# Cross-attention of a decoder layer: key tiles scored in pairs, another order of the work beside them, ten batches per loop iteration

## The chip, the cores and the metric

The kernel runs on one core of one Trainium2 chip. The metric is the time of one execution on the device in microseconds. The core's engines are TensorE (PE in the profile; its weight loads are PEld), VectorE (DVE), ScalarE (ACT), GpSimd (POOL), and SyncE (SP), which here only issues DMAs.

## The reference, cut to what matters

The layer is self-attention, cross-attention and a feed-forward block, each with a residual and a layernorm after it. The change is in the middle one. For 32 batches, 100 queries and 1444 keys of 256 features, 16 heads of 16:

```python
def _w8a8_linear(x, w, b):            # both sides rounded to whole numbers in -127..127
    qx, sx = _dyn_quant(x)
    qw, sw = _quant_weight(w)
    y = jnp.einsum('bnc,oc->bno', qx, qw) * (sx * sw[:, 0])
    return y + b
q = _w8a8_linear(x, wq, bq).reshape(B, N, H, D).transpose(0, 2, 1, 3)
k = (cond @ wk.T + bk).reshape(B, L, H, D).transpose(0, 2, 1, 3)
v = (cond @ wv.T + bv).reshape(B, L, H, D).transpose(0, 2, 1, 3)
scores = jnp.einsum('bhnd,bhld->bhnl', q, k) * inv_sqrt_d + mask[:, None]
attn = jax.nn.softmax(scores, axis=-1)
o = jnp.einsum('bhnl,bhld->bhnd', attn, v)
return _w8a8_linear(o.transpose(0, 2, 1, 3).reshape(B, N, C), wo, bo)
```

## The kernel before, in words

The three stages follow each other. Cross-attention works on one batch per turn. Its 1444 keys are 12 tiles of up to 128 (the last has 36 rows), its 16 heads four quads. A **unit** `("u", g, t)` is one key tile for one quad: four score matmuls with keys on the partitions (L1283), one exponential on ScalarE over 128 x 400 (L1098), and, two units later, four matmuls that add the weighted values to `acc` (L1246). There are 48 units in a turn. Scores go by turns into two PSUM banks, `unit0` and `unit1`, and exponentials into three slots of `prob`. Between the first and second score matmul of a unit TensorE branches on a flag that tells whether the mask is zero (L1287).

Keys and queries are float32 cut into three bf16 parts, stacked over 96 partitions; three more rows hold the negated row maximum, so that the scores come out already lowered. So the maxima must be known before the scores: for each head, `mh` (two matmuls of 512 keys) and `ml` (one of 420) make scores with queries on the partitions in `ca_rowmax` (L1163), VectorE reduces them (L1388), and per quad VectorE cuts the maximum in three parts, `mr` transposes these into a `unit` bank (L1172), and ScalarE copies them into the query stack (L1081).

Besides its own units a turn prepares the next batch and finishes the one before. `slots` names the tasks behind each unit, and every engine goes through the same list (`run_turns`), doing its part of each task:

- `ct` k c: four context tiles transposed on TensorE (L1210), copied by ScalarE (L1047).
- `kp` k c: key product of a third of the keys (L1129; its first half is `ka`); ScalarE writes the high part (L1056), VectorE the rest (L1347), `km` is ScalarE's middle part (L1063), and GpSimd makes the low part (L1002).
- `vp` j: value product of two tiles (L1136; first half `va`), with the bias added by VectorE into `ca_vaug` (L1362).
- `qq`, `qx`, `qp`, `qs`: quantise the next queries (VectorE), transpose, multiply, cut into parts on GpSimd, transpose the parts.
- `ma`, `mf`: is the next mask zero.
- `eo`, `ex`, `ey`: output of the batch before: divide and quantise, transpose, output product, residual and layernorm.

SP works through `step` once per batch: it loads the next context, then copies key parts from `ca_key_part` into the stack `ca_ks` as they become ready (L887, 24 copies), and doubles parts inside the stack (L893, L895), for heads 0 to 7 and then 8 to 15. `mh` 0 and `mh` 8 wait for these. It also loads queries, mask and residual and stores the result.

The counters of `Banks` order who writes and who frees a PSUM bank. The loop over batches holds two turns per iteration; the first and the last turn stand outside it, so it runs 15 times.

Of the kernel before, what the change touches and what calls it, by code (L numbers as in the profile page):

```python
# [19 lines left out]
P = 128  # L20
# [4 lines left out]
class Banks:  # L25
# [614 lines left out]
def cross_attention(nc, sems, x1, ctx_in, mask, wq, bq, wkT, bk_in, wvT, bv, wo, bo, x2):  # L640
# [48 lines left out]
    UNITS = NQ * TILES  # L689
    LAG = 2  # L690
    HALF = EARLY = H // 2
    slots = {}

    def place(u, *tasks):
        slots.setdefault(u, []).extend(tasks)
# [4 lines left out]

    place(-1, ("ct", 0, 0), ("ct", 0, 1))
    place(1, ("eo",), ("ka", 0, 0), ("kp", 0, 0))
    place(3, ("km", 0, 0), ("ct", 1, 0), ("ex",))
    place(4, ("ka", 0, 1), ("kp", 0, 1), ("ey",))
    place(5, ("ct", 1, 1))
    place(6, ("km", 0, 1))
    place(7, ("ka", 1, 0), ("kp", 1, 0), ("mh", 8))  # L710
    place(8, ("km", 1, 0))
    place(9, ("ml", 8), ("ka", 1, 1), ("kp", 1, 1), ("mr", 1))
    place(10, ("mh", 9), ("km", 1, 1), ("ct", 2, 0))
    place(11, ("ct", 2, 1), ("mh", 10))
    place(12, ("ml", 9), ("ka", 2, 0), ("kp", 2, 0))
    place(13, ("qq",), ("ml", 10), ("mh", 11))
    place(14, ("ka", 2, 1), ("kp", 2, 1))
    place(15, ("ml", 11))
    place(16, ("km", 2, 0), ("km", 2, 1), ("mh", 12))
    place(17, ("qx",), ("ml", 12), ("qp",))  # L720
    place(18, ("mh", 13), ("va", 0), ("vp", 0))
    place(19, ("ml", 13))
    place(20, ("mh", 14))
    place(21, ("ml", 14), ("va", 1), ("mr", 2), ("vp", 1))
    place(23, ("mh", 15), ("qs", 0))
    place(24, ("va", 2), ("ml", 15), ("vp", 2))
    place(25, ("qs", 1))
    place(27, ("mh", 0))
    place(28, ("va", 3))
    place(29, ("ml", 0), ("mh", 1), ("vp", 3))  # L730
    place(31, ("ml", 1), ("mh", 2))
    place(33, ("ml", 2), ("va", 4))
    place(34, ("mr", 3), ("mh", 3), ("vp", 4))
    place(36, ("ml", 3))
    place(37, ("mh", 4), ("va", 5), ("vp", 5))
    place(38, ("ma",))
    place(39, ("ml", 4))
    place(41, ("mh", 5))
    place(43, ("ml", 5))
# [1314 lines left out]
```

## Time and profile before

| | us |
|---|---|
| median of 3 runs | 4297.15 (4296.39 to 4300.14) |
| span of the profiled execution | 4293.6 |
| TensorE busy | 3851.9 (90%) |
| VectorE busy | 2586.9 (60%) |
| ScalarE busy | 1705.4 (40%) |
| GpSimd busy | 646.0 (15%) |

"Busy" adds up the instructions of an engine. The granted clock is the share of TensorE's full clock that it was given; 0.50 is 1.2 GHz and 1.00 is 2.4 GHz. "Issue" as a releaser means that the engine waited for nothing that the profile shows.

### The profile page before, as it was taken

The page shows a single profiled execution, that of the slowest core. Times are in us where ns is not written, and L with a number is a line of the kernel's source. Part 1 is how long each engine was busy: PE and PEld are TensorE (multiplying, and loading weights), DVE is VectorE, ACT ScalarE, POOL GpSimd, SP SyncE. Part 2 cuts the span into 40 slices and gives each one's busy share as a digit, 9 for nine tenths or more (in the row PEclk, how much of TensorE's full clock was granted, in tenths as well). Part 3 has the DMA queues.
Part 4 walks back from the last instruction along what each step waited for, and adds up shares of the span by engine and source line. Part 5 has one row for each costly group of instructions (what it writes and reads, how often), then busy time and mean ns, then how long its engine had stood idle before and what let it go on. Part 6 is the DMA issues. An engine that isn't in the chain of part 4 may idle for free. (4 is left out here: it accounts for less than half of the span.)

```text
span 4293.6 us, 98259 instructions
## 1 busy us (share of the span) xinstructions
PE 3851.9 (90%) x34364; PEld 2651.9 (62%) x34364; DVE 2586.9 (60%) x6225; ACT 1705.4 (40%) x3482; POOL 646.0 (15%) x784
## 2 busy tenths in 40 slices
PE   7999999966989889889889988988988987999998
PEld 6999999963555555555555555555555545666665
DVE  4444444454667666666666666666756745666665
ACT  3223222222444444444444544544544433333232
POOL 0000000021111011011111110110101102243222
PEclk9999999987999899999999999989999968999999
DMA  2000000014635436446445354454453411000000
GB/s 91 13 12 11 11 11 11 8 38 77 105 74 103 86 71 110 84 80 103 77 88 100 71 103 88 83 95 86 88 97 74 86 28 54 16 11 11 19 11 12
DMA packets 121851, 257.48 MB, mean 60 GB/s; under 512 B 18564, under 2 KB 99276, under 8 KB 118364
## 3 DMA queue, kind: packets, MB, share of 16 engines
q1 hardware_dynamic: 113136, 243.95, 30.2%
q10 hardware_dynamic: 8300, 7.69, 0.6%
q8 instruction: 297, 4.87, 0.5%
q14 instruction: 118, 0.97, 0.1%
HBM read 99.79 MB, written 9.83 MB: 26 GB/s over the span
## 5 line engine op out<-in xcount | busy, mean ns | idle before, releaser
L1388 DVE CUSTOM_DVE_ANT_0 ca_rowmax<-ca_rowmax,ca_msk 100x1024 f32<-100x1024 f32 (+1 forms) x1024 | 926.9, 924 | 460.9 <-PE ca_rowmax L1163 452.7
L1098 ACT ACTIVATE ca_prob<-ca_unit 128x400 f32<-128x400 f32 (+1 forms) x1536 | 759.0, 501 | 824.6 <-PE ca_unit L1283 802.4
L1163 PE MATMUL ca_rowmax<-ca_ks,ca_qs 96*100 96x512 bf16 (+1 forms) x1536 | 518.5, 407 | 155.9 <-DMA ca_ks<-ca_ks 78.3
L1283 PEld LDWEIGHTS ca_unit<-ca_qs,ca_ks 99*128 99x128 bf16 (+1 forms) x6144 | 413.5, 102 | 280.9 <-issue 177.7
L1246 PE MATMUL ca_acc<-ca_prob,ca_vaug 128*17 128x100 f32 x12288 | 576.9, 262 | 0.0
L1283 PE MATMUL ca_unit<-ca_qs,ca_ks 99*128 99x100 bf16 (+1 forms) x6144 | 569.3, 216 | 1.3 <-issue 0.3
L1002 POOL TENSOR_TENSOR ca_key_part<-ca_key_rest,ca_key_part 128x512 bf16<-128x512 f32 (+1 forms) x192 | 209.7, 1099 | 2028.8 <-ACT ca_key_part L1063 2028.8
L1136 PE MATMUL ca_ring<-ca_wvT,ca_ctxT 128*128 128x256 f32 (+1 forms) x1536 | 441.8, 419 | 0.4 <-DVE ca_vaug L1362 0.4
L1129 PE MATMUL ca_ring<-ca_ctxT,ca_wkT 128*128 128x512 f32 (+1 forms) x768 | 365.7, 600 | 3.9 <-DVE ca_key_rest L1347 2.2
L1163 PEld LDWEIGHTS ca_rowmax<-ca_ks,ca_qs 96*100 96x100 bf16 x1536 | 157.6, 128 | 323.3 <-issue 213.3
L1136 PEld LDWEIGHTS ca_ring<-ca_wvT,ca_ctxT 128*128 128x128 f32 (+1 forms) x1536 | 297.8, 202 | 84.1 <-issue 27.6
L1246 PEld LDWEIGHTS ca_acc<-ca_prob,ca_vaug 128*17 128x17 f32 x12288 | 205.8, 96 | 139.7 <-issue 14.4
L1347 DVE SCALAR_TENSOR_TENSOR ca_key_rest<-ca_ring,ca_bk_col,ca_key_part 128x512 f32<-128x512 f32 (+1 forms) x192 | 137.8, 717 | 190.1 <-ACT ca_key_part L1056 190.1
L1056 ACT ACTIVATE ca_key_part<-ca_ring,ca_bk_col 128x512 bf16<-128x512 f32 (+1 forms) x192 | 127.0, 661 | 245.3 <-PE ca_ring L1129 245.3
L313 ACT ACTIVATE sa_capped<-sa_ps 100x400 f32<-100x400 f32 x128 | 64.5, 504 | 402.3 <-PE sa_ps L419 402.3
L1210 PE MATMUL ca_ring<-ca_ident,ca_ctx 128*128 128x128 f32 (+1 forms) x768 | 138.5, 304 | 90.0 <-issue 86.9
L1129 PEld LDWEIGHTS ca_ring<-ca_ctxT,ca_wkT 128*128 128x128 f32 x768 | 140.9, 198 | 109.0 <-issue 104.2
L1210 PEld LDWEIGHTS ca_ring<-ca_ident,ca_ctx 128*128 128x128 f32 (+1 forms) x768 | 98.1, 153 | 136.6 <-issue 124.5
L86 PE MATMUL sa_ps<-sa_xT_hi,sa_w_hi 128*128 128x400 f32 x512 | 177.3, 346 | 0.0
L88 PE MATMUL sa_ps<-sa_xT_hi,sa_w_lo 128*128 128x400 f32 x512 | 175.0, 342 | 0.0
L259 POOL TENSOR_SCALAR_AFFINE_SELECT sa_causal<-sa_prob 100x400 f32<-100x400 f32 x128 | 69.3, 542 | 701.8 <-ACT sa_prob L320 701.8
L516 DVE COPY sa_kT<-sa_ps 128x400 f32<-128x400 f32 x128 | 73.5, 574 | 168.3 <-PE sa_ps L88 168.3
(258 smaller groups left out, 6549.7 us busy)
## 6 DMA issues: line engine op xcount, KB each, us to landing
ca_ks<-ca_key_part SPq DMA_DIRECT2D x768, 90.2 KB, 4.2
ca_ks<-ca_ks SPq DMA_DIRECT2D x64, 722.0 KB, 5.8
ca_ctx<-in_ctx SPq DMA_DIRECT2D x32, 1408.0 KB
ca_ks<-ca_ks SPq DMA_DIRECT2D x64, 361.0 KB, 8.8
ca_msk<-in_mask_BxSxS_ff SPq DMA_DIRECT2D x32, 564.1 KB
sa_w_stage<-in_L_attn_w_qkv SPq DMA_DIRECT2D x12, 512.0 KB, 5.2
sa_x_in<-in_x ACTq DMA_DIRECT2D x8, 400.0 KB
sa_x_res<-in_x SPq DMA_DIRECT2D x8, 400.0 KB
```

The lines of the kernel that those rows point to most:

```text
L86: pe.matmul(out, w_hi, x_hi, start=(start and n == 0), stop=False)
L88: last = pe.matmul(out, w_lo, x_hi, start=False, stop=(stop and n == len(pairs) - 1))
L1002: pool.tensor_tensor(key_part[:, 2, c, s], key_rest[:, n % 2, 0:w], key_part[:, 1, c, s], ALU.subtract).then_inc(parts_out, 1)
L1098: act.activation(prob[0:rows(t), u % 3, :], unit[bank][0:rows(t), 0:QUAD * N], ACT.Exp)\
L1129: return pe.matmul(ring[bn.bank(task)][:, 0:w], wkT_s[:, ci, c * P:(c + 1) * P], ctxT[:, ci, s], start=(ci == 0), stop=(ci == C - 1))
L1136: last = pe.matmul(ring[bn.bank(task)][0:rows(t), j * D:(j + 1) * D], ctxT[:, ci, t * TL:t * TL + rows(t)], wvT_s[:, ci, :], start=(ci == ...
L1163: last = pe.matmul(rowmax[0:N, s0:s1], qs[0:STACK, par, h, :], ks[0:STACK, par, h, s0:s1], start=True, stop=True)
L1210: last = pe.transpose(tile[:, n * TL:n * TL + rows(t)], ctx_t[0:rows(t), t, c * P:(c + 1) * P], ident[0:rows(t), 0:rows(t)])
L1246: last = pe.matmul(acc[32 * j:32 * j + DH + 1, g * N:(g + 1) * N], vaug[0:rows(t), par, t, head_at(g * QUAD + j), :], prob[0:rows(t), u % ...
L1283: return pe.matmul(unit[bank][0:rows(t), j * N:(j + 1) * N], ks[:, par, h, s], qs[:, par, h, :], start=(j == 0), stop=True, skip_group_che ...
L1347: dve.scalar_tensor_tensor(key_rest[:, n % 2, 0:w], ring[bank][:, 0:w], bk_col[:, c:c + 1], key_part[:, 0, c, s], ALU.add, ALU.subtract)\
L1388: dve.tensor_tensor_reduce(rowmax[0:N, s0:s1], rowmax[0:N, s0:s1], msk[:, par, s0:s1], 1.0, -3.0e38, ALU.add, ALU.max, top[:, bank, h:h + ...
```

## The change: what it does

It touches cross-attention alone.

- **Rounds of two tiles.** A turn has 24 pairs `("u", p)` in place of 48 units. `unit` becomes one PSUM tensor over two banks and is counted as one buffer, which the pairs and the `mr` tasks share. Eight score matmuls fill it, the branch on the mask stands ahead of the eighth, one activation over 128 x 800 makes the exponentials (two activations where the second tile has 36 rows), and the eight value matmuls of the pair before follow directly. `prob` has four slots.
- **Order of the tasks.** The `slots` table is written anew over rounds 0 to 24. The key products stand in rounds 1 to 8 (of 24), the value products in rounds 9 to 20. Their two halves are one task each, so `ka` and `va` are gone. Heads 0 to 5 of the next batch are scored for their maxima in rounds 16 to 23, heads 6 and 7 at the start of their own turn (before: 0 to 7 ahead of it). `mr` 1, 2, 3 and 0 stand in rounds 5, 11, 17 and 23, and rounds 12, 18 and 21 hold only `ml` 13, 1 and 3.
- **The end of a batch.** `ez` is new: the last layernorm step, in round 6, two rounds behind `ey`. The result is written in place (`res = summed`), so VectorE waits in `eo` until the batch before is stored.
- **Loop.** Ten turns per iteration, 3 iterations. Tasks that have no batch at the first and last turn are passed over by `skip_run`, which sets the counters.

SP's program is the same but for the count of pairs.

```diff
+    slots = {
+        ...
+        11: [("mr", 2), ("qx",), ("mh", 13), ("vp", 1), ("qp",)],
+        12: [("ml", 13)],
+        ...
+    }
-        unit = [ctx.enter_context(nc.psum_tensor(f"ca_unit{k}", [P, 512], F32)) for k in range(2)]
+        unit = ctx.enter_context(nc.psum_tensor("ca_unit", [P, 2, 512], F32))
-        bc = Banks(nc, sems, "ca_cur", cur_order, lambda t: cur_order.index(t) % 2)
+        bc = Banks(nc, sems, "ca_cur", cur_order, lambda t: 0, lag={t: 1 - batch_of(t) for t in cur_order})
-        prob = sb("prob", [TL, 3, QUAD * N])
+        prob = sb("prob", [TL, 4, QUAD * N])
-        res = sb("res", [N, 1, D])
+        res = summed
+        LOOP = 10
-            with eng.Fori(0, B // 2 - 1) as pair:
-                turn(2 * pair + 1, 1)
-                turn(2 * pair + 2, 0)
+            with eng.Fori(0, (B - 2) // LOOP) as n:
+                for k in range(LOOP):
+                    turn(LOOP * n + k + 1, (k + 1) % 2)
...
             def do_round(b, par, p):          # ScalarE
+                t, s = 2 * (p % PER_QUAD), slice(2 * (p % 2), 2 * (p % 2) + 2)
+                bc.wait_full(act, ("u", p), b)
+                if rows(t + 1) == TL:
+                    act.activation(prob[:, s, :], unit[:, :, 0:QUAD * N], ACT.Exp).then_inc(bc.freed[0], 1)
+                else:
+                    act.activation(prob[:, s.start, :], unit[:, 0, 0:QUAD * N], ACT.Exp)
+                    act.activation(prob[0:rows(t + 1), s.start + 1, :], unit[0:rows(t + 1), 1, 0:QUAD * N],
+                                   ACT.Exp).then_inc(bc.freed[0], 1)
...
             def do_round(b, par, p):          # TensorE
-                head(0)
+                for j in range(QUAD):
+                    head(0, j)
+                for j in range(QUAD - 1):
+                    head(1, j)
                 with pe.If(masked[par] != 0):
...
-                for j in range(1, QUAD):
-                    last = head(j)
-                last.then_inc(bc.filled[bank], 1)
-                if u >= LAG:
-                    weighted_values(b, par, u - LAG)
+                head(1, QUAD - 1).then_inc(bc.filled[0], 1)
+                if p:
+                    weighted_values(b, par, p - 1)
...
                 elif kind == "eo":            # VectorE
+                    dve.wait_ge(out_stored, 16 * b + 1)
...
                 elif kind == "ey":
-                    dve.wait_ge(out_stored, 16 * b + 1)
+                elif kind == "ez":
                     layernorm_apply(dve, summed, moments, rstd, res, 1, rstd_done, out_ready, b)
```

On TensorE, in the first turn, where `mr` 1 stands, before: two units (scores, branch, values), `ml` (100x420), a key product, `mr` into `unit1`, and the next scores into `unit0`.

```order
L1283 MATMUL ca_unit1<-ca_qs,ca_ks 128x100 x3
L1246 MATMUL ca_acc<-ca_prob,ca_vaug 17x100 x4
L1283 MATMUL ca_unit0<-ca_qs,ca_ks 128x100
L1287 COMPARE_AND_BRANCH
L1288 MATMUL ca_unit0<-ca_ident,ca_msk 128x400
L1287 UNCONDITIONAL_BRANCH
L1283 MATMUL ca_unit0<-ca_qs,ca_ks 128x100 x3
L1246 MATMUL ca_acc<-ca_prob,ca_vaug 17x100 x4
L1163 MATMUL ca_rowmax<-ca_ks,ca_qs 100x420
L1129 MATMUL ca_ring1<-ca_ctxT,ca_wkT 128x512 x2
L1172 MATMUL ca_unit1<-ca_ident_b,ca_top_part 3x100 x4
```

The same place now, round 5 (its second tile has 36 rows):

```order
L1283 MATMUL ca_unit<-ca_qs,ca_ks 128x100 x4
L1283 MATMUL ca_unit<-ca_qs,ca_ks 36x100 x3
L1290 COMPARE_AND_BRANCH
L1292 MATMUL ca_unit<-ca_ident,ca_msk 128x400
L1292 MATMUL ca_unit<-ca_ident,ca_msk 36x400
L1290 UNCONDITIONAL_BRANCH
L1283 MATMUL ca_unit<-ca_qs,ca_ks 36x100
L1246 MATMUL ca_acc<-ca_prob,ca_vaug 17x100 x8
L1168 MATMUL ca_unit<-ca_ident_b,ca_top_part 3x100 x4
L1159 MATMUL ca_rowmax<-ca_ks,ca_qs 100x512 x2
L1132 MATMUL ca_ring1<-ca_ctxT,ca_wkT 128x512 x2
```

Eight scores stand together, eight values behind them, and `mr` writes `unit` right behind these, which is the buffer that the eight scores have just filled.

On VectorE, around the quantising of the next queries (`ca_x_q` to `ca_x_int`), before. The rows that write `ca_rowmax` are the maxima of `mh` (100x1024) and `ml` (100x420).

```order
L1347 SCALAR_TENSOR_TENSOR ca_key_rest<-ca_ring0,ca_bk_col,ca_key_part 128x420
L632 TENSOR_REDUCE ca_x_st<-ca_x_q 100x1
L633 TENSOR_SCALAR ca_x_st<-ca_x_st 100x1
L634 RECIPROCAL ca_x_st<-ca_x_st 100x1
L635 TENSOR_SCALAR ca_x_sc<-ca_x_q,ca_x_st 100x256
L636 TENSOR_SCALAR ca_x_sc<-ca_x_sc 100x256
L637 TENSOR_SCALAR ca_x_int<-ca_x_sc 100x256
L1388 ISA ca_rowmax,ca_top<-ca_rowmax,ca_msk 100x420
L1388 ISA ca_top 100x1
L1388 ISA ca_rowmax,ca_top<-ca_rowmax,ca_msk 100x1024
```

And now, in round 10:

```order
L1391 ISA ca_rowmax,ca_top<-ca_rowmax,ca_msk 100x1024
L1391 ISA ca_top 100x1
L644 TENSOR_REDUCE ca_x_st<-ca_x_q 100x1
L645 TENSOR_SCALAR ca_x_st<-ca_x_st 100x1
L646 RECIPROCAL ca_x_st<-ca_x_st 100x1
L647 TENSOR_SCALAR ca_x_sc<-ca_x_q,ca_x_st 100x256
L648 TENSOR_SCALAR ca_x_sc<-ca_x_sc 100x256
L649 TENSOR_SCALAR ca_x_int<-ca_x_sc 100x256
L1391 ISA ca_rowmax,ca_top<-ca_rowmax,ca_msk 100x420
L1391 ISA ca_top 100x1
```

Ahead of it stands the maximum of `mh` 12 in place of a key rest, and only `ml` 12 is queued behind it before the next round.

## Rows read from the trace of the kernel before

**Rows 1.** The page: its span, and two groups of its part 5.
```profile
span 4293.6 us, 98259 instructions
...
L1246 PE MATMUL ca_acc<-ca_prob,ca_vaug 128*17 128x100 f32 x12288 | 576.9, 262 | 0.0
L1283 PE MATMUL ca_unit<-ca_qs,ca_ks 99*128 99x100 bf16 (+1 forms) x6144 | 569.3, 216 | 1.3 <-issue 0.3
```

**Rows 2.** Stretches: length, busy time by engine, granted clock, DMA share, GB/s.
```profile
1046.00:3529.00 2483.00, 2240.06 (x24324) 1343.10 (x24322) 1612.64 (x3865) 1167.23 (x2345) 304.64 (x341) 0.92 0.48 86
1138.04:1212.93 74.89, 69.14 (x767) 41.49 (x766) 51.17 (x123) 36.77 (x75) 9.84 (x12) 0.95 0.52 93
1212.93:1295.41 82.48, 70.41 (x767) 42.72 (x766) 51.39 (x123) 36.90 (x75) 9.85 (x12) 0.92 0.46 85
```

**Rows 3.** Timeline of SP's queue: context loads, first and last of 29.
```profile
1138.04 0.41 SPq L874 DMA_DIRECT2D ca_ctx<-in_ctx  x1
...
3336.51 0.40 SPq L874 DMA_DIRECT2D ca_ctx<-in_ctx  x1
```

**Rows 4.** TensorE's waits from 1117 to 3340: us in total, times, longest.
```profile
PE ca_ring L1210 <- issue: 86.9, 28, 4.1
PE ca_rowmax L1163 <- DMA ca_ks<-ca_ks: 72.0, 24, 4.5
PE ca_rowmax L1163 <- DVE ca_top L1388: 54.9, 56, 1.8
```

**Rows 5.** Timeline of TensorE at a loop end: start, length, [idle before].
```profile
1587.08 0.47 PE L1210 MATMUL ca_ring<-ca_ident,ca_ctx 128*128 128x128 f32 x1 [4.13 <-issue]
1590.00 1.76 PE L1210 MATMUL ca_ring<-ca_ident,ca_ctx 128*128 128x128 f32 x7 [2.46 <-issue]
```

**Rows 6.** Stretches behind a wait for VectorE and at that loop end.
```profile
1541.05:1544.46 3.41, 3.41 (x19) 2.16 (x19) 2.09 (x4) 0.50 (x1) 2.71 (x4) 0.50 1.02 149
1585.42:1595.66 10.24, 6.13 (x24) 4.21 (x25) 2.41 (x9) 1.99 (x4) 0.00 (x0) 0.50 0.07 24
```

**Rows 7.** Timeline of TensorE at the wait for a maximum.
```profile
1539.95 0.64 PE L1163 MATMUL ca_rowmax<-ca_ks,ca_qs 96*100 96x512 bf16 x2 [1.69 <-DVE ca_top L1388]
```

**Rows 8.** Timeline of TensorE without a wait, at the full clock.
```profile
1545.08 0.63 PE L1163 MATMUL ca_rowmax<-ca_ks,ca_qs 96*100 96x512 bf16 x2
1545.55 0.35 PE L1283 MATMUL ca_unit<-ca_qs,ca_ks 99*128 99x100 bf16 x4
1545.83 0.37 PE L1246 MATMUL ca_acc<-ca_prob,ca_vaug 128*17 128x100 f32 x8
1546.12 0.38 PE L1163 MATMUL ca_rowmax<-ca_ks,ca_qs 96*100 96x420 bf16 x1
1546.34 1.03 PE L1136 MATMUL ca_ring<-ca_wvT,ca_ctxT 128*128 128x256 f32 x4
1547.30 0.34 PE L1172 MATMUL ca_unit<-ca_ident_b,ca_top_part 100*3 100x100 bf16 x4
1547.57 1.13 PE L1136 MATMUL ca_ring<-ca_wvT,ca_ctxT 128*128 128x256 f32 x4
```

**Rows 9.** Timeline of all engines: a unit's scores and their exponential.
```profile
1578.77 0.34 PE L1283 MATMUL ca_unit<-ca_qs,ca_ks 99*128 99x100 bf16 x4
...
1579.23 0.50 ACT L1098 ACTIVATE ca_prob<-ca_unit 128x400 f32<-128x400 f32 x1 [0.15 <-PE ca_unit L1283]
```

**Rows 10.** Groups by form, ScalarE, 1117 to 3340: busy, mean ns of one.
```profile
L1074 ACT ACTIVATE ca_qs<-ca_ring 96x800 bf16<-96x800 bf16 x56 | 46.6, 832 | 23.8 <-PE ca_ring L1233 23.8
```

**Rows 11.** Timeline: last high part, SP's copies and doublings, first `mh`.
```profile
1533.81 0.61 ACT L1056 ACTIVATE ca_key_part<-ca_ring,ca_bk_col 128x420 bf16<-128x420 f32 x1 [1.32 <-PE ca_ring L1129]
...
1534.61 10.89 SPq L887 DMA_DIRECT2D ca_ks<-ca_key_part  x16
1547.88 0.52 SPq L893 DMA_DIRECT2D ca_ks<-ca_ks  x1
...
1557.53 0.63 PE L1163 MATMUL ca_rowmax<-ca_ks,ca_qs 96*100 96x512 bf16 x2 [2.22 <-DMA ca_ks<-ca_ks]
```

More of the change, by code:

```diff
@@ L57, in skip, with skip_run @@
         pe.sem_inc(self.freed[self.bank(tile)], 1)
+    def skip_run(self, pe, tiles, turn_of):
+        first, n = {}, {}
+        for tile in tiles:
+            bank = self.place[tile][0]
+            first.setdefault(bank, tile)
+            n[bank] = n.get(bank, 0) + 1
+        for bank, tile in first.items():
+            self.wait_empty(pe, tile, turn_of(tile))
+            pe.sem_inc(self.filled[bank], n[bank])
+            pe.sem_inc(self.freed[bank], n[bank])
     def wait_empty(self, eng, tile, turn):
@@ L711, in cross_attention @@
[L711 to L721, printed above, removed]
@@ L769, in cross_attention @@
+    cur_order = [t for t in timeline if t[0] in ("u", "mr")]
+    top_order = [t for t in timeline if t[0] in ("mh", "ml", "eo", "ex", "ey")]
     with ExitStack() as ctx:
@@ L952, in _, with run_turns, turn @@
             sp.wait_ge(out_stored, 16 * B + 1)
-        def run_turns(eng, do_task, do_round, skip=lambda task, turn: None):
-            def turn(b, par, first=False, last=False):
-                for u in ROUNDS:
-                    do_round(b, par, u)
-                    for task in slots.get(u, []):
+        LOOP = 10
+        assert (B - 2) % LOOP == 0 and LOOP % 2 == 0
+        def run_turns(eng, do_task, do_round, skip=lambda tasks, turn: None):
+            def turn(b, par, aheads=(-1, 0, 1)):
+                for p in ROUNDS:
+                    if 0 in aheads:
+                        do_round(b, par, p)
+                    for task in slots.get(p, []):
@@ L960, in turn @@
                         ahead = batch_of(task)
-                        if ahead == -1 and first:
-                            skip(task, -1)
-                        elif not (ahead == 1 and last):
+                        if ahead in aheads:
                             do_task(b + ahead, (par + ahead) % 2, task)
-            for task in timeline:
-                if batch_of(task) == 1:
-                    do_task(0, 0, task)
-            turn(0, 0, first=True)
-            with eng.Fori(0, B // 2 - 1) as pair:
-                turn(2 * pair + 1, 1)
-                turn(2 * pair + 2, 0)
@@ L973, in run_turns @@
-            turn(B - 1, 1, last=True)
-            for n in range(EARLY):
-                skip(("mh", n), B)
-            for task in end_tasks:
+                        elif ahead == -1:
+                            skip([task], b)
+            skip([t for t in timeline if batch_of(t) < 1], -1)
+            for p in ROUNDS:
+                for task in slots.get(p, []):
+                    if batch_of(task) == 1:
+                        do_task(0, 0, task)
+            turn(0, 0, aheads=(0, 1))
@@ L977, in run_turns @@
+            with eng.Fori(0, (B - 2) // LOOP) as n:
+                for k in range(LOOP):
+                    turn(LOOP * n + k + 1, (k + 1) % 2)
+            turn(B - 1, 1, aheads=(-1, 0))
+            ends = [t for t in timeline if batch_of(t) == -1]
+            skip([t for t in timeline if batch_of(t) == 1], B - 1)
+            skip(timeline[:timeline.index(ends[0])], B)
+            for n, task in enumerate(ends):
                 do_task(B - 1, 1, task)
+                if n + 1 < len(ends):
+                    skip(timeline[timeline.index(task) + 1:timeline.index(ends[n + 1])], B)
```

203 lines of the change are left out of this document (82 added, 121 removed), and 23 rows, old and new, of the table slots.

## The prediction, made before the changed kernel ran

> **What bounds the kernel now.** I read the busy time by stretch first, then the starts of the batches, then TensorE's waits, then its timeline at the waits, and last the queues that those waits name.
>
> The change touches only cross-attention. That stage is 2483 us of the 4293.6 us span [rows 1, 2]. In it TensorE is busy 2240 us, at a mean granted clock of 0.92, while VectorE has 1613 us and ScalarE 1167 us. So TensorE sets the pace, and what can be won is its idle time, its time at the lower clock, and the price of each of its steps.
>
> The load of the context tile is issued at the same place of every batch. From its row at 1138.04 to that at 3336.51 there are 28 batches, so 78.5 us each [rows 3]. They are not alike: one takes 74.89 us, the next 82.48 [rows 2]. The longer one has the end of the loop body in it. There TensorE stands still for 4.13 us and, one matmul later, for 2.46 us, with nothing that it waits for [rows 5]. The grouped row counts 86.9 us in 28 such places, two at each of 14 loop ends, so 6.2 us per end [rows 4]. Behind such a halt the granted clock is 0.50, which is 1.2 GHz, for 10.24 us, of which 6.13 us are work [rows 6]; at 2.4 GHz that work takes half, so 3.1 us more are lost. A loop end costs 6.2 + 3.1 = 9.3 us. Without one a batch is 78.5 - 9.3/2 = 73.8 us.
>
> In those 73.8 us TensorE waits 72.0/28 = 2.6 us for the stacked keys and 54.9/28 = 2.0 us for VectorE's row maxima [rows 4]. After such a wait (1.69 us here) the clock is 0.50 for 3.41 us [rows 6, 7], which costs 1.7 us of work; with two such waits in a batch, 3.4 us. Waits and their clock: 8.0 us a batch.
>
> **The change, part by part.**
>
> *Loop ends.* Two turns per iteration become ten: 15 iterations become 3, 14 loop ends become 2. Saved: 12 x 9.3 = 112 us. From below, with the idle time alone, it is 12 x 6.2 = 74 us; from above I see nothing dearer, since a batch's code streams once either way. In the second turn of today's body (74.89 us) no such halt shows, so ten turns in a row should show none.
>
> *Groups of eight.* Today four score matmuls start 0.28 us ahead of the value matmuls, and those 0.29 us ahead of the next step [rows 8]. Four scores span 0.35 us and one lasts 0.216 [rows 1, 8], so they start (0.35 - 0.216)/3 = 0.045 us apart; four such steps are 0.18, and 0.10 is left for the change to another group. The values span 0.37 with 0.262 for one, two passes some 0.11 apart, so 0.07 to 0.09 is left there. A pair of tiles drops one of each: 0.57 x 2 - 0.18 = 0.96 us instead of 1.14, and 24 pairs save 4.3 us a batch. The bounds are 0 (if the gap is the price of the weights, and not of the group) and 4.6. I take 4.0. Joining the two halves of the key and value products changes an order only, and I put it at nothing, as no work of theirs goes.
>
> *One score buffer in place of two.* The scores of a pair can be written only when the exponential of the pair before has been read out. ScalarE began 0.12 us after the scores' end (1578.77 + 0.34 to 1579.23) [rows 9]. An activation of 800 columns takes 0.832 us [rows 10], where today two of 400 take 0.50 each. Counted from the first score: last one starts at 7 x 0.045, ends 0.21 later, so 0.53; then 0.12 + 0.83; the buffer is free at 1.48. TensorE has scores and values for 0.96, so a round needs 0.5 us of other tasks to hide it. A matmul pair "mh" is 0.47, "ml" 0.22, a value product 2 x 0.96 [rows 8]. Most rounds have enough. Rounds 12, 18 and 21 hold one "ml" alone: 3 x (0.5 - 0.22) = 0.8 us. The four "mr" transposes now share that buffer and stand right behind the values: 4 x 0.5 = 2.0 us. Together +2.8 us a batch; the bounds are 0 (if ScalarE is quicker than the row of 800) and 24 x 0.5 = 12 us (no cover at all).
> The Trainium skill (Perfetto Trace Analysis, Matmuls) says that independent matmul groups should rotate through PSUM banks, so that read-out of one overlaps the next group. By that rule the one buffer is a loss in every round. The rows agree with the delay, but the tasks between the rounds are such other work.
>
> *Keys early, values late.* The chain behind the first "mh 0" is long: the last key product's high part is written at 1533.81 + 0.61 = 1534.42, SP then issues 16 copies (10.89 us), the two doubling copies follow at 1547.88, and the "mh" that needs them starts at 1557.53, after a wait of 2.22 us [rows 11]. That is 23.1 us from the high part, or 23.8 from the end of the product on TensorE (0.12 + 0.61 more). SP's program is the same, so this stays. After the change what lies between is rounds 9 to 15 and the pair of 16: eight pairs at 0.96 = 7.7, five "ml" 1.1, four "mh" 1.9, four value products 7.7, one "mr" 0.3, the query steps about 1.2 (an estimate from 20 short matmuls at the pitches above): 19.9 us. With waits of 0.5 (mr 2) and 0.3 (round 12), and 1.2 at the query transpose (below), 21.9. So about 1.9 us of wait stay, with one spell of the low clock, 1.7.
> VectorE quantises the queries in round 10, behind the maximum of mh 12, and the transpose that needs it stands in round 11, not four rounds on. I put 1.2 us there, between 0 and the 1.69 that TensorE waits behind the same work today [rows 7]. Queued behind that wait are mh 13 and value product 1. VectorE is busy 51.2 us in a batch [rows 2], so 0.73 of 70: tight, and 0.6 us of small waits for maxima in rounds 20 and 0 are added. The last layernorm step is a task of its own two rounds later, so VectorE no longer stands for GpSimd; off TensorE's path, nothing. The load of the mask flag had eight transposes to hide it and now stands ahead of the first scores: 0.3.
> Waits and clock after: 1.9 + 1.7 + 1.2 + 0.6 + 0.3 = 5.7, against 8.0: saved 2.3.
>
> **The sum.** A batch: -4.0 + 2.8 - 2.3 = -3.5 us, so 70.3. But the 0.8 us of score-buffer wait inside the key chain are already in its 1.9, and I do not take them out: they stand for what I have not seen. 31 turns hold all this work: 31 x 3.5 = 108 us. Of the other turn and the head of the stage nothing is counted; to be cautious I take 100. 4293.6 - 112 - 100 = 4082 us of span. The shown median is 4297.15, 3.5 above the span of the profiled execution, so 4085 us.
>
> **The rivals.**
> 1. *The body breaks even.* The group change is worth 0 to 1, and the buffer and VectorE eat it; only loop ends are won: 4297 - 112 = 4185. For it: VectorE at 0.73 and a chain of 23.8 us that no order shortens. Against it: the wait total of 8.0 us shrinks by the row sums. The same time comes if the order pays but long straight code halts where the short body did not.
> 2. *All waits close.* The chain is covered and the low clock with it: 70.3 - 1.9 - 1.7 - 0.7 = 66.0, so 31 x 7.8 + 112 = 354, 3943 us.
> 3. *Slower: the single score buffer keeps the clock down.* Each short wait on it, 7 a batch, opens a spell of 3.41 us at 1.2 GHz. 7 spells more than I count cost 7 x 1.7 = 12 us a batch, 370 in all: 4455. It decides from 212/31/1.7 = 4.0 more spells a batch. For it: 1.69 us of waiting did this. Against it: these waits are under a third of that, and nothing in the rows shows one so short doing it.
> The Trainium skill (Perfetto Trace Analysis, Optimizing Scalar/DVE Operations) holds that where ScalarE is not saturated but causes bubbles elsewhere, instructions are to be broken up, not merged. It speaks for rivals 1 and 3: ScalarE is at 0.49 here [rows 2].
>
> **How the numbers follow.** My forecast, 4085 with its own range of 4020 to 4160, has 0.50. Rival 1, 4160 to 4230, 0.22. Rival 2, 3940 to 4020, 0.15. Rival 3 has 0.10, and other losses 0.03. Leaving out a part of rivals 2 and 3 gives 3975 to 4225. A change under 0.2%, some 9 us, cannot be told from none. Faster 0.86, same 0.02, slower 0.12.
>
> **What would show it.** Right: two pairs of halts at loop ends instead of 14; batches without one at 69 to 72 us; eight scores starting 0.45 to 0.5 us ahead of their values; an exponential of 0.83 us; waits of TensorE for ScalarE's exponential of some 0.5 us ahead of "mr" and about 0.3 in rounds 12, 18, 21; a wait of 1 to 3 us for the stacked keys. Wrong: waits for the exponential in most rounds, a granted clock in the stage below 0.92, halts without a releaser inside the straight code, or row maxima that TensorE waits for by more than 2 us a batch.

## The result: 4101 us, 4.6% faster

The changed kernel takes 4101.48 us, the median of 4 runs (4087.13 to 4115.7), against 4298.65 us (4296.39 to 4303.73) for the kernel before. The ratio is 0.9537, 95% interval 0.9511 to 0.9562. The forecast was 4085. Twelve more runs follow; the last is the changed kernel again, at 4100.13.

The profiled execution is the longest of the four, 4115.7 us with a span of 4114.0. Nine of its microseconds are lost in self-attention, which the change does not touch: that part is 946 us long before and 955 here. So sizes below are compared by the stretch of cross-attention, from its first score to its last value. Before, [rows 2] have it in 2483 us, 2 of which lie outside the first score and the last value. The changed kernel's stage and one of its batches, with the columns of [rows 2]:

```profile
1053.30:3347.20 2293.90, 2069.76 (x24333) 1357.19 (x24333) 1625.93 (x3872) 1057.52 (x1705) 306.93 (x341) 0.94 0.52 93
1461.00:1535.00 74.00, 66.23 (x776) 43.26 (x775) 51.77 (x123) 33.37 (x54) 9.90 (x11) 0.93 0.51 94
```

The stage is 187 us shorter. Length less TensorE's busy time is its idle time: from the first score to the last value it is 242 us before and 224 after. So only some 18 us come from less waiting and 170 from less work time of TensorE, although it has as many matmuls as before. That work time is shorter steps, and 12 loop ends without their stretch at the half clock.

The first and the last of 29 context loads (SP's queue; minimum, median and maximum of the duration in ns, then first and last start) are 2030.7 us apart, 72.5 us a batch against 78.5 [rows 3]:

```profile
L865 SPq DMA_DIRECT2D ca_ctx<-in_ctx x29: 394/395/411, 1145.0 to 3175.7; - x29
```

TensorE's waits from 1117 to 3150, with the columns of [rows 4]:

```profile
PE ca_unit L1168 <- ACT ca_prob L1100: 58.6, 112, 0.6
PE ca_ring L1220 <- DVE ca_x_int L649: 37.1, 28, 1.6
PE ca_rowmax L1159 <- DMA ca_ks<-ca_ks: 36.6, 21, 2.8
PE ca_acc L1246 <- issue: 20.5, 7, 4.0
PE ca_rowmax L1159 <- DVE ca_top L1391: 14.7, 28, 0.5
PE ca_unit L1283 <- issue: 14.6, 30, 4.2
```

Of the 86.9 us at loop ends 11 are left, at two ends; the key wait is halved, the wait for maxima is 15 us in place of 55. In their place stand two new waits that had been forecast, for the exponential ahead of `mr` (L1168) and for the quantised queries (L1220), and one that had not: halts in the middle of the value matmuls (L1246) for which the list names no releaser.

The timeline shows the new rounds. TensorE, start, length, [idle before]:

```profile
1514.52 0.53 PE L1283 MATMUL ca_unit<-ca_qs,ca_ks 99*128 99x100 bf16 x8
1514.98 0.54 PE L1246 MATMUL ca_acc<-ca_prob,ca_vaug 128*17 128x100 f32 x16
1515.45 0.81 PE L1159 MATMUL ca_rowmax<-ca_ks,ca_qs 96*100 96x512 bf16 x3
...
1516.66 0.54 PE L1246 MATMUL ca_acc<-ca_prob,ca_vaug 128*17 128x100 f32 x16
1517.78 0.34 PE L1168 MATMUL ca_unit<-ca_ident_b,ca_top_part 100*3 100x100 bf16 x4 [0.58 <-ACT ca_prob L1100]
1519.41 0.25 PE L1220 MATMUL ca_ring<-ca_ident_b,ca_x_int 100*128 100x100 bf16 x2 [1.29 <-DVE ca_x_int L649]
...
1522.39 0.66 PE L1246 MATMUL ca_acc<-ca_prob,ca_vaug 128*17 128x100 f32 x16
1522.98 0.38 PE L1159 MATMUL ca_rowmax<-ca_ks,ca_qs 96*100 96x420 bf16 x1
1523.39 0.53 PE L1283 MATMUL ca_unit<-ca_qs,ca_ks 99*128 99x100 bf16 x8
...
1535.69 1.44 PE L1159 MATMUL ca_rowmax<-ca_ks,ca_qs 96*100 96x512 bf16 x3 [2.77 <-DMA ca_ks<-ca_ks]
...
1847.35 0.84 PE L1283 MATMUL ca_unit<-ca_qs,ca_ks 99*128 99x100 bf16 x8 [4.12 <-issue]
1849.40 1.09 PE L1159 MATMUL ca_rowmax<-ca_ks,ca_qs 96*100 96x512 bf16 x2 [1.20 <-issue]
...
1902.89 0.33 PE L1246 MATMUL ca_acc<-ca_prob,ca_vaug 128*17 128x100 f32 x1 [3.95 <-issue]
```

Eight scores start 0.46 us ahead of their values and those 0.47 ahead of the next step: 0.93 us a pair in place of 1.14 [rows 8]. Behind them the list has each foreseen wait once, then a loop end (1847.35 and 1849.40), and 55 us later a halt of 3.95 us inside one pair's values. Such a halt comes twice in each loop iteration, at the same two places: at 1174.63, 1462.02, 1902.89, 2188.79, 2628.49 and 2918.95, of 2.9 to 4.0 us (a seventh place in the row above has 0.4).

The DMA queues tell what may be missing there. The page names queue 8 "instruction"; it moves packets of 16 KB, about one in 10 us. In the stretch of each of the six halts exactly one of them starts. From 1898.94 to 1902.89 (packets, MB, share):

```profile
q8 instruction: 1, 0.02, 1.6%
```

In all six TensorE starts again 1.5 to 1.9 us after this packet's end; shifted by 3, 5 or 7 us the six restarts would meet two packets so at most. Before, all 28 stops at loop ends end in the same way, 1.2 to 1.9 us after such a packet. So both are most likely waits for the next piece of the program. Why it comes late at just these places no run settles.

The key chain, on ScalarE and on SP's queue:

```profile
1511.85 0.61 ACT L1057 ACTIVATE ca_key_part<-ca_ring,ca_bk_col 128x420 bf16<-128x420 f32 x1 [1.61 <-PE ca_ring L1132]
```

```profile
1512.66 11.91 SPq L878 DMA_DIRECT2D ca_ks<-ca_key_part  x16
1525.58 0.52 SPq L884 DMA_DIRECT2D ca_ks<-ca_ks  x1
```

From the high part's end at 1512.46 to the `mh` 0 at 1535.69 it is 23.2 us, as long as before [rows 11]. The DMA engines are busy for 0.86 of the time in which SP issues the 16 copies. The stretch behind that wait, and the same stage's longest group on ScalarE from the page:

```profile
1535.65:1542.48 6.83, 6.54 (x39) 4.31 (x40) 3.13 (x6) 1.38 (x3) 0.00 (x0) 0.50 0.65 114
```

```profile
L1097 ACT ACTIVATE ca_prob<-ca_unit 128x800 f32<-128x800 f32 x640 | 534.6, 835 | 558.7 <-PE ca_unit L1283 558.6
```

The granted clock is 0.50 (1.2 GHz) for 6.83 us behind the key wait, twice the spell of [rows 6]. Such a spell, a stretch at 0.50 without a break, is not new: before, too, 26 of the 32 outside loop ends in 28 batches last 6.83 us, and only 6 last 3.41. A key wait's spell before, and the spell of the halt at 1902.89:

```profile
1165.58:1172.41 6.83, 5.25 (x32) 3.13 (x33) 1.29 (x2) 1.01 (x2) 0.00 (x0) 0.50 0.64 109
1900.88:1911.12 10.24, 7.98 (x42) 5.04 (x42) 3.14 (x6) 1.38 (x3) 0.00 (x0) 0.50 0.74 127
```

Each of the six halts has such a spell of 10.24 us. The exponential takes 835 ns, where 832 had been taken over from [rows 10].

### The profile page after: what moved, and what is told of

Read it like the earlier page. It is cut to its first block and busy times, and to the rows that moved or that the text cites. A ratio compares the mean times of both kernels' runs of the same rounds, so it can differ in the third digit from the quotient of the medians.

```text
span 4114.0 us, 95372 instructions
## 1 busy us (share of the span) xinstructions
PE 3691.4 (90%) x34364; PEld 2671.0 (65%) x34364; DVE 2596.5 (63%) x6225; ACT 1596.1 (39%) x2842; POOL 648.8 (16%) x784
## 5 line engine op out<-in xcount | busy, mean ns | idle before, releaser
L1097 ACT ACTIVATE ca_prob<-ca_unit 128x800 f32<-128x800 f32 x640 | 534.6, 835 | 558.7 <-PE ca_unit L1283 558.6
L1283 PEld LDWEIGHTS ca_unit<-ca_qs,ca_ks 99*128 99x128 bf16 (+1 forms) x6144 | 356.0, 100 | 212.2 <-issue 124.8
L1246 PE MATMUL ca_acc<-ca_prob,ca_vaug 128*17 128x100 f32 x12288 | 444.6, 258 | 21.1 <-issue 20.8
L1283 PE MATMUL ca_unit<-ca_qs,ca_ks 99*128 99x100 bf16 (+1 forms) x6144 | 439.4, 212 | 24.1 <-issue 15.3
L1141 PE MATMUL ca_ring<-ca_wvT,ca_ctxT 128*128 128x256 f32 (+1 forms) x1536 | 418.2, 419 | 0.9 <-ACT ca_qs L1075 0.6
L1141 PEld LDWEIGHTS ca_ring<-ca_wvT,ca_ctxT 128*128 128x128 f32 (+1 forms) x1536 | 314.9, 207 | 79.7 <-issue 17.8
L1132 PE MATMUL ca_ring<-ca_ctxT,ca_wkT 128*128 128x512 f32 (+1 forms) x768 | 346.1, 573 | 2.3 <-ACT ca_ctxT L1048 2.3
L1246 PEld LDWEIGHTS ca_acc<-ca_prob,ca_vaug 128*17 128x17 f32 x12288 | 235.2, 98 | 110.0 <-issue 48.3
L1365 DVE TENSOR_TENSOR ca_vaug<-ca_ring,ca_bias_row 128x512 f32<-128x512 f32 (+2 forms) x224 | 134.6, 613 | 97.2 <-PE ca_ring L1141 96.4
L99 PE MATMUL sa_ps<-sa_xT_lo,sa_w_hi 128*128 128x400 f32 x512 | 174.4, 341 | 0.0
```

The source lines that it names most:

```text
L99: pe.matmul(out, w_hi, x_lo, start=False, stop=False)
L1097: act.activation(prob[:, s, :], unit[:, :, 0:QUAD * N], ACT.Exp).then_inc(bc.freed[0], 1)
L1132: last = pe.matmul(ring[bn.bank(task)][:, 0:w], wkT_s[:, ci, c * P:(c + 1) * P], ctxT[:, ci, s], start=(ci == 0), stop=(ci == C - 1))
L1141: last = pe.matmul(ring[bn.bank(task)][0:rows(t), j * D:(j + 1) * D], ctxT[:, ci, t * TL:t * TL + rows(t)], wvT_s[:, ci, :], start=(ci == ...
L1246: last = pe.matmul(acc[32 * j:32 * j + DH + 1, g * N:(g + 1) * N], vaug[0:rows(t), par, t, head_at(g * QUAD + j), :], prob[0:rows(t), 2 * ...
L1283: return pe.matmul(unit[0:rows(t0 + k), k, j * N:(j + 1) * N], ks[:, par, h, keys(k)], qs[:, par, h, :], start=(j == 0), stop=True, skip_g ...
```

## The experiments

All are edits of the changed kernel, except the second. Each was timed in 4 runs, beside the kernel before on the same chip (medians there 4296.97 to 4301.7). "Changed" is 4101 us.

**1. The changed kernel with two turns per iteration.** What is the new order worth without the long body?

```diff
-        LOOP = 10
+        LOOP = 2
```

> The changed kernel with two turns per loop iteration again (LOOP = 2), all else as changed. Theory A (a loop end costs 9.3 us, and the seven halts without a releaser that the changed kernel shows inside its straight code, 2.9 to 4.0 us each, come with the length of the loop body): 12 loop ends more, 112 us, less six halts with the low clock behind them, some 5 us each: about 4183 us, 14 loop ends in the trace and no halt elsewhere. Theory B (the halts come with the new order of the instructions and stay): about 4213 us. Theory C (a loop end costs little in this order of the work, since what TensorE loses it would have waited for the stacked keys anyway): under 4150 us.

4216.02 us (4207.45 to 4228.97), ratio 0.9803 [0.9774, 0.9832]. The 12 loop ends cost 115 us against the changed kernel, 9.5 each, where 9.3 was forecast. But nine more halts come with them (15 in the stage, against six): 20 us more of idle time, and some 45 us with the work at the half clock behind them. Without these an end is worth 6 to 8 us. Against the kernel before, the order and the pairs alone win 83 us. TensorE's waits:

```profile
PE ca_unit L1283 <- issue: 54.7, 28, 4.4
...
PE ca_acc L1246 <- issue: 33.3, 13, 3.7
```

The halt in the value matmuls (L1246) is here too, 13 times in this row, once an iteration, 55 to 57 us behind the restart at a loop end. So it is not a price of a long body: the two-turn body has it in every iteration.

**2. The kernel before with ten turns per iteration.** What is the long body worth without the new order?

```diff
-            with eng.Fori(0, B // 2 - 1) as pair:
-                turn(2 * pair + 1, 1)
-                turn(2 * pair + 2, 0)
+            with eng.Fori(0, (B - 2) // 10) as n:
+                for k in range(10):
+                    turn(10 * n + k + 1, (k + 1) % 2)
```

> The kernel before with ten turns per loop iteration, nothing else changed. Theory A: 12 loop ends at 9.3 us go, two halts in the straight code per iteration come: 4299 - 112 + 30 = about 4217 us. Theory B (no halts in the old order of instructions): 4187 us. Theory C (a loop end is worth less than 9.3 us): above 4240 us.

4216.53 us (4214.93 to 4217.8), ratio 0.9807 [0.979, 0.9823]: 82 us won, 6.8 per loop end and not 9.3.

```profile
PE ca_rowmax L1163 <- DMA ca_ks<-ca_ks: 86.8, 27, 4.2
PE ca_ring L1210 <- issue: 12.4, 4, 3.9
```

In this window there are four halts without a releaser, two at each of two loop ends, and none in straight code. Ahead of it, in the first turn, straight code of the old order halts once:

```profile
1094.24 1.06 PE L1163 MATMUL ca_rowmax<-ca_ks,ca_qs 96*100 96x512 bf16 x2 [3.37 <-issue]
```

No instruction packet ends ahead of this restart as at the others (one runs from 1093.34 to 1094.62), so its cause is open. The time that theory A had named came, but not by its six halts. Of the 30 us that are missing at least 15 went to the key wait: 87 us in 27 places, where the kernel before has 72 in 24 [rows 4]. A loop end had given the key chain time in some batches, and without it the chain ends last in all of them. The two parts are not additive: alone 83 and 82 us, together 197.

**3. The two banks of the score buffer counted apart.** Each tile has its own exponential of 400 columns again, and `mr` needs the first bank only.

```diff
+    cur_order = singles(...)          # ("u", p, 0), ("u", p, 1); mr in the first bank
                 for k in range(2):                               # ScalarE
+                    bc.wait_full(act, ("u", p, k), b)
+                    act.activation(prob[0:rows(t + k), s.start + k, :], unit[0:rows(t + k), k, 0:QUAD * N],
+                                   ACT.Exp).then_inc(bc.freed[k], 1)
...
                 for k in range(2):                               # TensorE
+                    if k:
+                        bc.wait_empty(pe, ("u", p, 1), b)
+                    head(k, QUAD - 1).then_inc(bc.filled[k], 1)
```

> The changed kernel with the two PSUM banks of a pair counted apart: an exponential of 400 columns and a release for each tile, the scores in two groups of four with a branch each, the eight values still together, mr in the first bank. My theory: the waits for the exponential (2.1 us a batch ahead of mr, 0.1 elsewhere) go, and one group change more per pair (0.09 us x 24 = 2.2 us) comes: within 15 us of the changed kernel's 4101. Rival (one buffer for two banks is what holds the changed kernel, and each wait drags the clock down): faster by 60 to 120 us. Rival (group changes are dearer than 0.09 us): slower by over 30 us.

4059.37 us (4049.55 to 4064.81), ratio 0.9438 [0.9417, 0.9459]: 42 us less than changed, between the 15 us of my theory and the 60 of the rival. Stage and waits:

```profile
1047.40:3291.10 2243.70, 2037.19 (x24333) 1351.47 (x24333) 1628.60 (x3872) 1093.39 (x2345) 306.37 (x341) 0.96 0.53 95
```

```profile
PE ca_ring L1221 <- DVE ca_x_int L649: 57.7, 29, 2.2
PE ca_rowmax L1160 <- DMA ca_ks<-ca_ks: 34.3, 19, 3.7
PE ca_rowmax L1160 <- DVE ca_summed L1427: 25.2, 29, 0.9
PE ca_rowmax L1160 <- DVE ca_top L1393: 22.5, 64, 0.5
```

The 58.6 us ahead of `mr` are gone, but 48 come back at VectorE's work (L1221 +21, `ca_summed` +19, `ca_top` +8). Idle time falls only from 224 to 207 us. The larger part is in the busy time, 33 us less at a clock of 0.96 instead of 0.94. The low clock goes chiefly behind the key wait: in 28 batches it has 10 spells there, 58 us, where the changed kernel has 15, 106 us, although the waits themselves are nearly the same (34.3 and 36.6 us). That the waits of half a microsecond had held the clock down is my reading; no run separates them from the other shifts.

**4. Queries quantised two rounds earlier.**

```diff
-        8: [("mh", 11), ("kp", 2, 1), ("km", 2, 0)],
+        8: [("mh", 11), ("qq",), ("kp", 2, 1), ("km", 2, 0)],
-        10: [("mh", 12), ("qq",), ("ml", 12)],
+        10: [("mh", 12), ("ml", 12)],
```

> The changed kernel with the quantising of the next queries in round 8, behind mh 11, in place of round 10. My theory: the 1.3 us that TensorE waits for it in round 11 of every batch go, but the first mh of round 16 still waits for the stacked keys, whose chain is as long as before, so that wait grows from 1.3 us a batch to about 2.5; what is won is at most the low clock behind one of two waits: 0 to 50 us, 4050 to 4100 us. Rival (the keys are not what ends last; every wait removed is won): 28 x (1.3 + 1.7) = 85 us, about 4016 us.

4117.25 us (4116.69 to 4121.94), ratio 0.9579 [0.9563, 0.9595]: 16 us more than changed, where 0 to 50 less were expected.

```profile
PE ca_rowmax L1159 <- DMA ca_ks<-ca_ks: 54.0, 22, 3.7
PE ca_rowmax L1159 <- DVE ca_top L1391: 31.4, 56, 0.8
```

The query wait of 37 us is gone. The key wait grew by 17 and that for maxima by 17. The query wait stood inside the key chain, and the chain ends last whether TensorE waits early or late.

**5. Value product 4 ahead of `mh` 0.** More independent work over the key chain.

```diff
-        16: [("mh", 0), ("ml", 0)],
-        17: [("mr", 3), ("mh", 1), ("vp", 4), ("mf",)],
+        16: [("vp", 4), ("mh", 0), ("ml", 0)],
+        17: [("mr", 3), ("mh", 1), ("mf",)],
```

> The changed kernel with value product 4 moved from round 17 to the head of round 16, ahead of mh 0, so that 1.9 us more of work lie over the stacking of the keys. My theory: the wait for the stacked keys (36.6 us over 28 batches) goes, and the low clock behind it in part: 35 to 75 us faster than the changed kernel, 4025 to 4065 us, with the wait for the queries left as it is. Rival (the time comes back as waits for the row maxima, since VectorE holds six heads in what is left of the turn): within 15 us of 4101.

4035.54 us (4029.14 to 4053.67), ratio 0.9393 [0.9363, 0.9424]: 66 us less than changed, for a wait of 36.6 us, of which 31.6 go. Stage, and what is left of the key wait:

```profile
1040.20:3269.90 2229.70, 2034.70 (x24333) 1330.28 (x24333) 1623.52 (x3872) 1057.31 (x1705) 306.29 (x341) 0.96 0.53 96
```

```profile
PE ca_rowmax L1159 <- DMA ca_ks<-ca_ks: 5.0, 8, 1.2
```

Here too the busy time fell (35 us) beside the idle time (29 us), and the clock is 0.96. The spell of the low clock goes with the wait: behind the key wait 2 of 15 are left.

**6. Experiments 3, 4 and 5 together.**

> The kernel with two banks counted apart (4059 us), with the quantising of the queries in round 8 and value product 4 ahead of mh 0 as well. My theory: with the stacking covered, the early quantising is worth its wait too (57.7 us over 28 batches there), and the low clock shrinks further: 3960 to 4010 us. Rival (waits for the row maxima take their place): 4040 to 4060 us.

4034.99 us (4018.46 to 4038.26), ratio 0.9374 [0.9349, 0.9399]: no better than experiment 5 alone, and above the 3960 to 4010 expected.

```profile
1043.80:3266.60 2222.80, 2055.15 (x24333) 1348.78 (x24333) 1640.96 (x3872) 1096.98 (x2345) 306.79 (x341) 0.97 0.52 96
```

```profile
PE ca_rowmax L1160 <- DVE ca_top L1393: 61.3, 105, 1.6
PE ca_rowmax L1160 <- DVE ca_summed L1427: 25.2, 29, 0.9
```

Waits for the exponential and the queries are gone, those for the keys are 3.5 us, and TensorE waits 86 us for VectorE's maxima and sums instead: 1641 of 2223 us busy, in a fixed order. The clock is higher than in experiment 5, yet TensorE's busy time is 20 us longer. They lie in the score matmuls, which alone grow by more: 484.5 us busy in the whole execution, against 435.9 in experiment 5. The next section has where this comes from.

**7 and 9. What the group change consists of.** In experiment 3 the eight scores are two groups of four, with a branch, a wait and an increment between. Experiment 7 also puts each half of the values behind its own wait; experiment 9 instead puts an increment that nobody waits for behind the first four values.

```diff
-                for k in range(2):
-                    bc.wait_out(pe, ("u", p, k), b)
+                    bc.wait_out(pe, ("u", p, k), b)      # 7: inside the loop over the two tiles
```

```diff
+                    if k == 0:
+                        last.then_inc(pe_passed, 1)      # 9: at the end of the first tile's values
```

> The kernel with two banks counted apart (4059 us), with the eight values of a pair in two groups of four, each behind its own wait for its exponential; nothing else differs, and those waits are long met. It measures one group change by itself: 32 x 24 = 768 more of them. By the rows of before, 0.07 to 0.09 us each: 54 to 69 us slower, 4113 to 4128 us. Rival (the gap belongs to the weights and not to the group): within 15 us of 4059.

> The kernel with two banks counted apart (4059 us); the last of a pair's first four value matmuls increments a spare semaphore for which nobody waits. Nothing else differs. Splitting the eight with a wait cost nothing, so the 0.09 us between groups are not the wait's. Theory A (they belong to the increment at a group's end): 768 more of them, 69 us slower, about 4128 us, and the second tile's values start 0.17 us behind the first's last pass and not 0.086. Theory B (they belong to the change of data type or bank): within 15 us of 4059.

7: 4065.41 us (4062.03 to 4071.33), ratio 0.9456 [0.9439, 0.9473]. 9: 4063.53 us (4059.58 to 4072.2), ratio 0.9463 [0.9447, 0.9478]. Both lie 4 to 6 us above experiment 3, at the edge of its spread, and their waits are the same to some 9 us (queries 57.7 us in both, keys 25.2 and 26.4). TensorE in experiment 7:

```profile
1500.85 0.54 PE L1284 MATMUL ca_unit<-ca_qs,ca_ks 99*128 99x100 bf16 x8
1501.31 0.54 PE L1247 MATMUL ca_acc<-ca_prob,ca_vaug 128*17 128x100 f32 x16
```

In experiment 7 eight scores still span 0.54 and start 0.46 ahead of the values, although they stand in two groups now, and the values span 0.54 as well. For the values this holds on average too: their busy time in the whole execution is 440.9 us in experiment 3, 440.1 with the wait and 443.1 with the increment. So neither costs anything that shows there. For the scores it does not hold. Their rows on the pages of the changed kernel and of experiments 3 and 6:

```profile
L1283 PE MATMUL ca_unit<-ca_qs,ca_ks 99*128 99x100 bf16 (+1 forms) x6144 | 439.4, 212 | 24.1 <-issue 15.3
L1285 PE MATMUL ca_unit<-ca_qs,ca_ks 99*128 99x100 bf16 (+1 forms) x6144 | 467.9, 211 | 29.1 <-issue 26.6
L1285 PE MATMUL ca_unit<-ca_qs,ca_ks 99*128 99x100 bf16 (+1 forms) x6144 | 484.5, 211 | 33.1 <-issue 28.6
```

The second group, with its branch, wait and increment, adds 28.5 us in experiment 3, 0.04 us for each of 768 pairs. The loss is uneven. From the first score to the values it is 0.465 us in the median against 0.458, but 0.53 against 0.48 in the mean, since some pairs lose 0.1 us or more at the fourth, fifth or eighth score, near the branches.

The 0.1 us between scores and values is another matter, and neither the wait nor the increment is its cause. Nor is it the step from bf16 to float32. In the changed kernel:

```profile
1512.58 0.38 PE L1159 MATMUL ca_rowmax<-ca_ks,ca_qs 96*100 96x420 bf16 x1
1512.79 1.89 PE L1141 MATMUL ca_ring<-ca_wvT,ca_ctxT 128*128 128x256 f32 x8
```

From this bf16 `ml` to the float32 value product it is 0.21 us, and 0.19 from an `ml` to bf16 scores (1508.66 to 1508.85). From the value product to the bf16 scores at 1514.52 it is 1.73, eight passes of 0.216. But `mr`, bf16 and with 3 columns of weights, costs 0.1 us ahead of it and 0.1 behind it [rows 8], and it does so ahead of a bf16 `mh` as well: 0.27 for four passes 0.043 apart (before, 1178.11 to 1178.38). In every place that I compared the gap stands between matmuls with 17 or 3 columns of weights and others with 36 to 128. No run tests the width by itself.

**8. Thirty turns per iteration.** No loop end is left.

```diff
-        LOOP = 10
+        LOOP = 30
```

> The changed kernel with all 30 middle turns in one iteration. Theory A (the halts without a releaser in the straight code belong to places at fixed distances behind a loop end): the two loop ends go (19 us) and four of the six halts with them (20 us): about 4060 us. Theory B (they belong to the order of the instructions and come twice in every ten turns): the halts stay, 4082 us.

4073.05 us (4067.31 to 4076.5), ratio 0.9469 [0.9453, 0.9485]: 28 us less than changed, between the 4060 and 4082 of the theories. The remaining halts:

```profile
PE ca_acc L1246 <- issue: 8.1, 5, 3.2
```

They are fewer and shorter (20.5 us before this edit; one more, of 1.4 us, stands behind the window at 3168.26), and at other places. A different place of the same code, with the order of instructions unchanged, moves them.

**10 and 11. The best parts joined.** 10 is experiment 5 with `LOOP = 30`, 11 is experiment 6 with it.

> Value product 4 ahead of mh 0 (4036 us), with all 30 middle turns in one iteration. If the 28 us that the long loop gave the changed kernel (two loop ends, fewer halts in the straight code) add up with it: 4005 to 4012 us. If what it gave was only an earlier clock recovery that the covered keys already have: 4020 to 4036.

> Two banks counted apart, queries and value product 4 early (4035 us), with one iteration: 4007 if the gain of the long loop adds up. The wait for the row maxima (61 us over 28 batches) should stay.

10: 4008.55 us (3995.29 to 4018.13), ratio 0.9321 [0.9296, 0.9347], 27 less than experiment 5: it adds up. 11: 3989.27 us (3975.31 to 3996.47), ratio 0.9281 [0.9256, 0.9306], the fastest of all, 112 us below the changed kernel. It is 46 below experiment 6, more than the 28 that the loop had given and below the 4007 expected; the scores alone are busy 27.6 us less (456.9 for 484.5). Waits of experiment 11:

```profile
PE ca_rowmax L1160 <- DVE ca_top L1393: 67.9, 110, 1.2
PE ca_rowmax L1160 <- DVE ca_summed L1427: 31.2, 30, 1.4
PE ca_acc L1248 <- issue: 13.9, 5, 3.6
```

What is left are above all 99 us of waits for VectorE and 14 of halts.

**12. The changed kernel again.** No edit, on the chip of experiments 9 to 11; 1 to 8 ran on two others.

> The changed kernel once more, unedited, as the measure for the differences of 15 to 60 us between its variants: 4085 to 4116 us. If it comes out near 4117, the early quantising alone (4117 us) made no difference.

4100.13 us (4097.73 to 4106.16), ratio 0.9544 [0.9528, 0.956]. The medians of the changed kernel agree to 1.4 us, and those of the kernel before to 5 us over the three chips, so the larger comparisons above do not hang on the chip. The profiled execution of this run took 4099.6 us, near the median:

```profile
1043.30:3333.10 2289.80, 2063.48 (x24333) 1354.69 (x24333) 1625.55 (x3872) 1057.53 (x1705) 306.66 (x341) 0.94 0.52 93
```

Against it TensorE's busy time falls by 26 us in experiment 3 and 29 in experiment 5, and its idle time by 20 and 31.

## Why the prediction came out right

The time was 16 us above the forecast and inside its own range. That the sum is close rests in part on errors of both signs.

**Loop ends: the sum right, in part by luck.** Two are left of 14, with 5.3 us idle in the one shown (4.12 + 1.20). In the new order each is worth 9.5 us, against 9.3 forecast, but up to 3.7 of these belong to the halts that come with each iteration (experiment 1), which the forecast did not have. In the old order experiment 2 gives 6.8: there the key wait takes a part back. And the 9.3 was read at an end with 10.24 us of low clock, which 8 of the 14 have; the others have 6.83. Idle time and work at the half clock over all 14 make 8.8.

**Groups of eight: right, at the upper bound.** Clean pairs save 0.21 us each, 5.0 us for 24. By busy time it is less: 170 us, less the half-clock work of 12 loop ends (12 x 3.1 = 37 [rows 6]), is 133 us, 4.3 a batch. The forecast took 4.0 and had 4.3 by the rows. Its bounds asked whether the gap belongs to the group or to the weights. By experiments 7 and 9 it belongs to neither the wait nor the increment of a group, but to the change between kinds of matmul; what goes with it is the width of the weights.

**One score buffer: right.** `mr` waits 0.58 us instead of 0.5, four times a batch: 58.6/28 = 2.1 us, forecast 2.0. With one `ml` between, values and next scores are 0.41 + 0.59 us apart (1522.39, 1522.98, 1523.39). Elsewhere an `ml` followed by scores takes 0.19 (1508.66 to 1508.85) or 0.22 (experiment 3, 1507.29 to 1507.51), so some 0.2 is waiting, less than the 0.28 forecast. In no other round does a wait of over 0.2 us for it show. The mask flag costs (14.6 - 2 x 4.2)/28 = 0.2 (L1283 without a releaser, less two loop ends), forecast 0.3.
The rule of the Trainium skill (Perfetto Trace Analysis, Matmuls) that independent groups should rotate through PSUM banks is borne out in direction by experiment 3, which also halves each exponential: with the banks counted apart the kernel is 42 us faster. It is no loss in every round, since all but 7 of 24 are covered.

**Keys, queries, maxima: right in kind.** The key chain kept its 23.2 us (23.1 before), and its wait is 36.6/28 = 1.3 us a batch, forecast 1.9. The query transpose waits 37.1/28 = 1.3, forecast 1.2. The maxima cost 14.7/28 = 0.5, forecast 0.6. That the chain, and not the query wait, ends last is shown by experiments 4 and 5.

**The clock: the mis-sized term.** The working let the low clock fall from 3.4 to 1.7 us a batch, since one of two waits of over a microsecond goes. Time at the half clock follows from the stage's rows as (1 - clock) x 2 x length: 397 us before and 275 after. Without 12 loop ends (8.8 us of low clock each, the mean of the 14) before has 292, so outside the loop ends it hardly fell. The record of the granted clock over the 28 batches shows why. Before, it is 321 us: 123 at the loop ends and 198 in 32 other spells. That is about one spell of 6.83 us a batch and not two of 3.41; its price, 198/28/2 = 3.5 us, agrees with the 3.4 of the working by two errors that cancel. After, it is 225 us: 17 at the loop ends, 61 behind the six halts, and 147 in 27 other spells. These cost 147/28/2 = 2.6 us and not 1.7, since behind the key wait 12 of 15 last 6.83 us. That lost 0.9 us a batch. Only three of the 27, 10 us together, have no wait of 0.9 us or more just ahead of them, so of rival 3's mechanism, short waits that open such spells by themselves, hardly anything shows.

**Halts in straight code: not in the sum.** The forecast had named them as what would show it wrong, and in rival 1's last sentence. They came six times, 20 us, and with half of the 53 us of work at the half clock behind them they cost 47 us, more than the forecast is off. Experiment 1 shows that the body's length does not make them, experiment 2 that the old order has one too, in its first turn, and experiment 8 that they move and shrink when the same instructions stand at other places. That TensorE lacks instructions there is likely from the packets of queue 8; why they come late stays open.

**The ledger.** A batch without loop ends was forecast at 70.3 us. Measured it is (2030.7 - 16 - 47)/28 = 70.3, without the two loop ends (11 us idle and half of 10 us of work at the half clock) and the halts. From -3.5: groups -0.3, clock behind waits +0.9, keys -0.6 give -3.5 again. Single terms are not that certain. So the batch came as forecast, by errors of both signs, and the halts are what lies above it. The 8 us that the sum held back, and some 9 more that the turns outside the 28 won, took a part of them in.

**Rival 2** (the chain fully covered, 3943) did not come, but experiments 5, 10 and 11 went that way: one value product moved wins 66 us. Covering it fully made VectorE late, as the 0.73 of its busy share had suggested.

## What to carry to other kernels

Put matmuls of one kind in a row: a change of kind costs some 0.1 us each time, more than a wait already met or an increment, and a branch among them costs now and then. Find the one chain that ends last in a batch (here DMA copies of 23 us) and lay independent work over it; shortening any other wait inside it gives nothing, as experiment 4 shows. Price a wait of TensorE above its own length, since the clock returns with it: here 66 us where 31.6 us of waits went. And read the price of a low clock from many spells, not from one: the one in [rows 6] was half as long as most. An unrolled body is a cheap way to lose loop ends, but measure it together with the order it is to carry, because a loop end may be hiding a chain.

## What the hardware showed that I had not expected

- TensorE halts of 1.2 to 4.5 us in straight code, without any releaser: in the changed kernel twice per ten-turn iteration, always at the same two places (+55 and +341 us), in experiment 1 once in each two-turn iteration, in experiment 2, in the old order, once at all. All six in the changed kernel end 1.5 to 1.9 us after a packet of the instruction queue.
- Matmuls of 17 or 3 columns of weights and wider ones cost some 0.1 us at each change between them; a change between bf16 and float32 alone does not show (0.21 us against 0.19). A wait already met or an increment between value matmuls does not show either (440.1 and 443.1 us busy against 440.9), while a second group of scores with its branch costs 0.04 us in the mean.
- The length of a spell at 1.2 GHz is not fixed: 3.41, 6.83 or 10.24 us here, 6.83 behind most waits for the keys, 10.24 behind each halt.
- The changed kernel spreads more from run to run than the kernel before: 4087 to 4116 against 4296 to 4304. In its longest run self-attention too, with the same code, was 9 us longer.
